# Self attention's projections as float16 pairs, with a reordered start and end, in a three-layer transformer block

## The reference, cut to what matters

```python
x = x + _L0_xattn_ref(_layernorm(x), ctx_1024, mask, rms_scale, q_w, kv_w, out_w)  # 32 x 64 rows, 512 wide
x = x + _L0_attn_ref(_layernorm(x), WQ, WK, WV, WO)
x = x + _L0_ffn_ref(_layernorm(x), W_fc, ln_w, ln_b, W_proj)
...
def _L0_attn_ref(x, WQ, WK, WV, WO):
    def heads(W): return (x @ W).reshape(B, S, 16, 32).transpose(0, 2, 1, 3)
    Q, K, V = (heads(WQ), heads(WK), heads(WV))
    score = causal softmax of einsum('bhqd,bhkd->bhqk', Q, K) / sqrt(32)
    out = einsum('bhqk,bhkd->bhqd', score, V)
    return out.transpose(0, 2, 1, 3).reshape(B, S, E) @ WO
```

## Time and profile before

| | us |
|---|---|
| median of 3 runs | 1067.03 (1064.93 to 1068.35) |
| profiled execution | 1066.37 |
| its span, first to last instruction | 1064.4 |
| TensorE busy, weight loads busy | 930.7, 700.7 |
| VectorE, ScalarE, GpSimd busy | 668.4, 505.0, 375.6 |

### The profile page before, as it was taken

How to read it: one execution, slowest core, us unless ns; L and a number is a source line. 1 busy time by engine, 2 the same in 40 slices (tenths; PEclk the granted TensorE clock), 3 DMA queues, 4 the chain that set the end, 5 groups by cost and what they waited for, 6 DMA issues and landing times. The chain is left out here.

```text
span 1064.4 us, 22549 instructions
## 1 busy us (share of the span) xinstructions
PE 930.7 (87%) x7307; PEld 700.7 (66%) x7307; DVE 668.4 (63%) x1334; ACT 505.0 (47%) x1059; POOL 375.6 (35%) x506
## 2 busy tenths in 40 slices
PE   3798879898888888878979999999889999999996
PEld 2787667686676776657968887888765444444443
DVE  5577756766766777676366566766656538475543
ACT  4565445654455554544333333433446455555542
POOL 3354444444444444440022111211103325444434
PEclk9899989999999999988989999999989999999998
DMA  6621223211222322331355543444422102012011
...
DMA packets 100318, 93.02 MB, mean 87 GB/s; under 512 B 45424, under 2 KB 61904, under 8 KB 100176
## 3 DMA queue, kind: packets, MB, share of 16 engines
...
q0 software_dynamic: 128, 0.03, 0.0%
...
## 5 line engine op out<-in xcount | busy, mean ns | idle before, releaser
L255 PE MATMUL bank<-f,f 128*128 128x256 f32 (+4 forms) x5032 | 637.8, 300 | 68.8 <-issue 26.0
L255 PEld LDWEIGHTS bank<-f,f 128*128 128x128 f32 (+3 forms) x5032 | 460.9, 160 | 196.5 <-issue 80.8
L244 DVE TENSOR_TENSOR f<-bank,f 128x512 fp32r<-128x512 f32 x211 | 140.5, 683 | 47.7 <-ACT f L241 45.8
L241 ACT ACTIVATE f<-bank 128x512 fp32r<-128x512 f32 x211 | 121.1, 591 | 88.8 <-PE bank L230 83.6
L230 PE MATMUL bank<-f,f 128*128 128x128 f32 x896 | 132.5, 279 | 33.7 <-DVE f L244 13.0
L230 PEld LDWEIGHTS bank<-f,f 128*128 128x128 f32 x896 | 102.9, 143 | 56.1 <-issue 31.3
L1248 PE MATMUL bank<-f,f 128*128 128x512 f16 x512 | 123.1, 384 | 0.0
L1221 POOL TENSOR_TENSOR f<-f,f 128x512 f32<-128x512 f32 x59 | 75.1, 1273 | 132.9 <-ACT f L1216 132.9
L1226 DVE SCALAR_TENSOR_TENSOR f<-bank,f,f 128x512 f16<-128x512 f32 x64 | 48.0, 750 | 92.0 <-ACT f L1208 75.8
L463 POOL TENSOR_TENSOR f<-f,f 128x512 f32<-128x512 f32 x32 | 42.0, 1311 | 160.9 <-ACTq L75 138.9
L954 POOL TENSOR_TENSOR f<-f,f 128x512 f32<-128x512 f32 x32 | 33.4, 1043 | 177.4 <-DVE f L951 177.4
...
## 6 DMA issues: line engine op xcount, KB each, us to landing
...
```

Source lines behind the costliest of these rows:

```text
L241: return maybe("act", lambda e: e.activation(hi, src, ACT.Copy), sem(name + "_hi"), waits, when)
L244: return maybe("dve", lambda e: e.tensor_tensor(lo, src, hi.bitcast(F32), ALU.subtract), sem(name + "_lo"), waits, when)
L255: f = lambda e, i=i, a=a, b=b: e.matmul(dst, a, b, start=(first and i == 0), stop=(last and i == n - 1), skip_group_check=check)
```

## The change

*Projections.* The pairs of WK, WQ, WV, WO, of the transposed x and of the attention result are float16 in place of float32r. Each weight is divided by its largest magnitude before it is split: `s2_wmax` reduces it on VectorE, `s2_wout` writes the 128 maxima to memory and `s2_wback` reads them back into every partition, `s2_wscale` takes the maximum and its reciprocal. Q and K are scaled back in ScalarE's copy out of PSUM (`s2_qk`), V times WO in `store`. `halves` is `split` without the bit cast; `s2_ET` uses it too. The split of WK moves from slots T0-6..T0-3 to T0-4..T0-1, the load of WO from B2+3 to T0+14.

*Start.* The squares of batches 0 to 2 move from three slots ahead of their tile's transpose to just behind it; the low part of the cross attention's Q weight moves from ahead of the slots into slots -1 and 0; Q2 and Q3 of pair 0 move from slots -3 and -1 to 1 and 3; the load of x for pair 1 moves from slot -4 to behind the first batch's loads; the first two masks are loaded behind the second batch's.

*End.* The last statistics stand ahead of all of the last two blocks' products, the sums of squares first; those products then run tile by tile.

The diff, without the passing of `wmaxd` (a 4x128 array in memory) from `program`, the `chunks` argument of `scaled_lo`, the type of `ET2` and its `halves`, and the removed line that emitted two of the last products ahead of the statistics:

```diff
             done["ssq", b] = done["sq"]
+            if b <= 2:
+                cx_free[b].append(done["sq"])
             tp = inv_sqrt("s_r", rr[:, b % 4, :], sst[:, b % 4, :], ss[:, b % 4, :],
...
         if j == FT - 1:
-            cx_free[b] = [tt, done["ssq", b]]
+            cx_free[b] = [tt, *([done["ssq", b]] if b > 2 else [])]
...
+    def first_masks():
+        for b in range(2):
+            done["msk", b] = load_mask(b)
     def stage_mask(b):
         u = b % 2
-        t = load_mask(b)
+        t = done["msk", b] if b < 2 else load_mask(b)
         done["bias", b] = [op("pool", lambda e: e.tensor_scalar(
...
     stage_Q1b(0)
-    tw1["q"] = scaled_lo(wq_t, WQh, WQl, [t_wq, t_r1], t_qh)
     side[0] = Q
     ahead = [(s, s.n) for s in sems.values()]
+    def stage_WQ(c):
+        tw1["q"] = scaled_lo(wq_t, WQh, WQl, [t_wq, t_r1], t_qh, [c])
     begun = [*begun, *(None if k.startswith("s_e_") else s.n for k, s in sems.items())]
     for c in range(4):
+        at(-1 + c // 2, 4, lambda c=c: stage_WQ(c))
         at(5 + c, 9, lambda c=c: stage_Wo(c))
     at(3, 9, load_wo)
+    at(-11, 2.65, first_masks)
     for b in range(nb):
...
         at(s0 - 6 if b > 2 else -11, 1.6 + b, lambda b=b: load_tab(b))
-        at(s0 + 4 if b > 0 else -1, 1.7, lambda b=b: stage_mask(b))
+        at(s0 + 4, 1.7, lambda b=b: stage_mask(b))
         for j in range(FT):
-            at(s0 - 5 + j, 0.3, lambda b=b, j=j: stage_square(b, j))
+            at(s0 - (5 if b > 2 else 2) + j, 0.3 if b > 2 else 1.5, lambda b=b, j=j: stage_square(b, j))
             at(s0 + j - 2, 1, lambda b=b, j=j: stage_T(b, j))
...
             if i:
-                at(s0 - 12, 1.4, lambda i=i: load_xq(i))
+                at(s0 - 12 if i > 1 else -11, 1.4 if i > 1 else 1.65, lambda i=i: load_xq(i))
                 at(s0 - 7, 1.4, lambda i=i: stage_Q0(i))
             if i:
                 at(s0 - 6, 8.1, lambda i=i: stage_Q1(i))
                 at(s0 - 5, 8, lambda i=i: stage_Q1b(i))
-            at(s0 - 3, 8, lambda i=i: stage_Q2(i))
-            at(s0 - 1, 8, lambda i=i: stage_Q3(i))
+            at(s0 - 3 if i else 1, 8, lambda i=i: stage_Q2(i))
+            at(s0 - 1 if i else 3, 8, lambda i=i: stage_Q3(i))
...
     for i in range(3):
-        Wh[i], Wl[i] = early(4, D, dt=F32R), early(4, D, dt=F32R)
-    XT = [early(2, 4, 256, dt=F32R), early(2, 4, 256, dt=F32R)]
+        early.at = CONST + (24576, 32768, 57344)[i]
+        Wh[i], Wl[i] = early(4, D, dt=F16), early(4, D, dt=F16)
+    early.at = CONST + 73728
+    XT = [early(2, 4, 256, dt=F16), early(2, 4, 256, dt=F16)]
+    early.at = CONST + 90112
     xa, xn = early(2, D), early(2, D)
-    Wh[3], Wl[3] = outs(4, D, dt=F32R), outs(4, D, dt=F32R)
+    Wh[3], Wl[3] = outs(4, D, dt=F16), outs(4, D, dt=F16)
     WO_raw = outs(4, D)
...
     mrow, mdiag, isc, sc, lsc = const(2), const(2), const(2), const(2), const(2, 16)
+    wmx, wis, wsc = const(4), const(4), const(5)
+    back = Region(CONST + EARLY + 72704, CONST + EARLY + 74752)(4, 128)
     tok, tW = {}, {}
...
+    def s2_wmax(i):
+        tok["wm", i] = op("dve", lambda e: e.tensor_reduce(
+            wmx[:, i:i + 1], raw_w(i).rearrange("p c n -> p (c n)"), AX.X, ALU.max, apply_absolute_value=True),
+            sem("s_wm"), [tok["w", i]])
+    def s2_wout(i):
+        tok["wo", i] = dma(wmaxd[i:i + 1, :].rearrange("a (p n) -> (a p) n", n=1), wmx[:, i:i + 1], f"s_wo{i}", [tok["wm", i]])
+    def s2_wback(i):
+        tok["wb2", i] = dma(back[:, i, :], wmaxd[i:i + 1, :].to_broadcast([128, 128]), f"s_wo{i}", [tok["wo", i]])
+    def s2_wscale(i):
+        D_ = lambda f, w: op("dve", f, sem("s_wm"), w)
+        t = D_(lambda e: e.tensor_reduce(wis[:, i:i + 1], back[:, i, :], AX.X, ALU.max), [tok["wb2", i]])
+        t = D_(lambda e: e.tensor_scalar(wis[:, i:i + 1], wis[:, i:i + 1], 1.0e-30, None, ALU.max), [t])
+        t = D_(lambda e: e.reciprocal(wsc[:, i:i + 1], wis[:, i:i + 1]), [t])
+        if i == 3:
+            t = D_(lambda e: e.tensor_tensor(wsc[:, 4:5], wis[:, 2:3], wis[:, 3:4], ALU.mult), [t])
+        tok["wsc", i] = t
     def s2_wsplit(i, after, c):
-        tW[i] = split("s_W2", raw_w(i)[:, c, :], Wh[i][:, c, :], Wl[i][:, c, :],
-                      [tok["w", i], *after()], [tok["w", i]])
+        src, hi, lo = raw_w(i)[:, c, :], Wh[i][:, c, :], Wl[i][:, c, :]
+        th = op("act", lambda e: e.activation(hi, src, ACT.Copy, scale=wsc[:, i:i + 1]), sem("s_W2_hi"),
+                [tok["wsc", i], *after()])
+        tl = op("dve", lambda e: e.scalar_tensor_tensor(lo, src, wsc[:, i:i + 1], hi, ALU.mult, ALU.subtract),
+                sem("s_W2_lo"), [th, tok["wsc", i]])
+        tW[i] = [th, tl]
+    def halves(name, src, hi, lo, w_hi, w_lo=()):
+        th = op("act", lambda e: e.activation(hi, src, ACT.Copy), sem(name + "_hi"), w_hi)
+        return th, op("dve", lambda e: e.tensor_tensor(lo, src, hi, ALU.subtract), sem(name + "_lo"), [th, *w_lo])
...
         tok["xnT", i] = [tt]
-        tok["XT", i] = split("n_XT", dst, dsth, dstl, [tt, *free])
+        tok["XT", i] = halves("n_XT", dst, dsth, dstl, [tt, *free])
         give(k, tok["XT", i])
     def store(i, dst_d, k, tk):
         u, j = i % 2, i % ni
-        to = op("dve", lambda e: e.tensor_tensor(xo[:, u, :], bank[k][:, :], xr[:, u, :], ALU.add),
-                sem("n_xo"), [tk, tok["xr", i], *tok["late"], *d2("ost", i - 2)])
+        to = op("dve", lambda e: e.scalar_tensor_tensor(xo[:, u, :], bank[k][:, :], wsc[:, 4:5], xr[:, u, :],
+                                                        ALU.mult, ALU.add),
+                sem("n_xo"), [tk, tok["xr", i], tok["wsc", 3], *tok["late"], *d2("ost", i - 2)])
         tok["out", i] = [to]
...
         o = (QT, KT)[which][:, u % 2, c, :]
-        tok["qk", u] = [op("act", lambda e: e.activation(o, bank[k][:, 0:256], ACT.Copy), sem("a_QK"),
-                           [tk, *tW[w], *tok["early"], *d2("sc", 2 * u - 3)])]
+        tok["qk", u] = [op("act", lambda e: e.activation(o, bank[k][:, 0:256], ACT.Copy, scale=wis[:, w:w + 1]), sem("a_QK"),
+                           [tk, tok["wsc", w], *tW[w], *tok["early"], *d2("sc", 2 * u - 3)])]
         give(k, tok["qk", u])
...
     at(T0 - 9, 0, s2_x)
-    at(T0 - 10, 2, lambda: s2_wload(0))
-    at(T0 - 6, 2, lambda: s2_wload(1))
-    at(T0 - 5, 2, lambda: s2_wload(2))
+    for i, s in enumerate((T0 - 10, T0 - 6, T0 - 5, T0 + 14)):
+        at(s, 2 if i < 3 else 8.8, lambda i=i: s2_wload(i))
+        at(s + 2, 9, lambda i=i: s2_wmax(i))
+        at(s + 3, 3, lambda i=i: s2_wout(i))
+        at(s + 4, 3, lambda i=i: s2_wback(i))
+        at(s + 6, 8.9, lambda i=i: s2_wscale(i))
     for c in range(4):
-        at(T0 - 6 + c, 9, lambda c=c: s2_wsplit(0, lambda: d("Q", ni - 1), c))
+        at(T0 - 4 + c, 9, lambda c=c: s2_wsplit(0, lambda: d("Q", ni - 1), c))
         at(T0 + 1 + c, 9, lambda c=c: s2_wsplit(1, lambda: done["kv", FT * nb - 1], c))
...
     at(T0 + 13, 8.9, s2_late)
-    at(B2 + 3, 8.7, s2_outs)
-    at(B2 + 3, 8.8, lambda: s2_wload(3))
+    at(T0 + 14, 8.7, s2_outs)
     for n in range(64):
...
     def s3_plast():
-        for t in (2, 3):
-            s3_p(last - 1, [t])
         for t in range(4):
-            s3_p(last, [t])
+            for q in (last - 1, last):
+                s3_p(q, [t])
     def s3_stat(g):
         v, k = g % 2, take()
-        w = [*tok["acc", g], *tok["acc2", g], *gfree[k], t_on]
-        for t in range(4):
-            for z in range(2):
+        w = {1: [*tok["acc2", g], *gfree[k], t_on], 0: tok["acc", g]}
+        for z in (1, 0):
+            for t in range(4):
                 rows = slice(t * 128, (t + 1) * 128)
                 parts = [acc[:, v, z, rows]] + ([sq3[:, last % 2, rows]] if z and g == ng - 1 else [])
                 for n, a in enumerate(parts):
                     tk = op("pe", lambda e, t=t, z=z, a=a, n=n, m=len(parts) - 1: e.matmul(
                         bank[k][:, z * 4 + t:z * 4 + t + 1], a, ones[:, 0:1], start=n == 0, stop=n == m,
-                        skip_group_check=True), sem("f_p") if t == 3 and z and n == len(parts) - 1 else None,
-                        w if t + z == 0 else ())
+                        skip_group_check=True), sem("f_p") if t == 3 and not z else None,
+                        w[z] if t + n == 0 else ())
         tok["stat", g] = [tk]
```

15 lines of the change are left out of this document (8 added, 7 removed).

## The result

The changed kernel takes 1078.31 us (median of 4 runs, 1075.47 to 1080.85) where the kernel before took 1066.64 beside it (4 runs). The recorded ratio is 1.0117, 95% interval 1.0098 to 1.0136; the two medians alone give 1.0109. It is slower by 1.1 to 1.2%. I had forecast 1050.0, with 1060 as the upper bound. The profiled execution took 1075.47 us, its span is 1073.5 us and its mean granted clock 0.965; before, 1066.37, 1064.4 and 0.970.

A forecast was written before the change was run, and what follows sets the result against it. It took TensorE to bound self attention and feed-forward. Projections -14, maxima +3.5 and +0.5, start -6, end -0.5 sum to -16.5 us from 1066.37: 1049.9, predicted as 1050.0 us, with 1038 to 1060 for 8 in 10.

The forecast's parts named there:

- Projections: Self attention: float16 groups save 21 us of TensorE time, of which 14 us are kept (7 to 21).
- Reductions: Passage to self attention: 2.3 us each on VectorE; +3.5 us on the path, plus 0.5 for the output weight.
- The small DMAs: SyncE's queue: the maxima's write makes Q and V weights some 3 us later; at nothing, up to 2 us.
- The start: First 45 us: early x for pair 1 removes 7 us of TensorE loss, 6 kept (2 to 8).
- the output weight's landing: Start: ScalarE would stall 4 to 5 us for the cross attention's output weight, about 4 us covered.
- WO's earlier load: Self attention's output weight loaded four slots earlier, its reduction hidden in VectorE's idle time; 0.5 us booked.
- The end: Last 20 us: statistics 0.7 us earlier, ahead of the last products; gain 0.5 us (0 to 0.8).
- (c): Passage: VectorE becomes the bound, reductions and landings waited for cost 18 us; 1073 us in all, chance 0.05.

The follow-up runs named there:

- run 4: The kernel before with only the edits to the first slots (squares, masks, x for pair 1, Q of pair 0); 1069.6 us, ratio 1.0034.
- run 7: The constant-scale kernel of run 3 with the load of WO back from slot T0+14 to B2+3; 1056.1 us, ratio 0.9907.
- run 3: The changed kernel with a constant scale of 16 for every weight, so no maxima, write or read back; 1061.7 us, ratio 0.9969.
- run 1: The changed kernel without the write of the maxima to memory and their read back, the four large reductions kept; 1065.9 us, ratio 0.9999.
- eleventh kernel: The constant-scale kernel of run 7 with the squares of batch 2 back at their old, early place; 1052.2 us, ratio 0.9879.
- run 5: The start-only kernel of run 4 with the squares of batch 2 back at their old place; 1063.2 us, ratio 0.9976.
- run 9: The start-only kernel of run 4 with pair 2's statistics of x queued on GpSimd behind r of batch 2; 1064.45 us, ratio 0.9988.
- eighth kernel: The changed kernel with each partition writing its maximum as 512 bytes instead of 4, one row read back; 1066.05 us, ratio 0.9994.

## Why the prediction was wrong

By the medians, a chain of single edits leads from before to after: 1065.7, + 3.9 (start, run 4), - 13.5 (projections and end, run 7 against run 4), + 5.6 (WO's place, run 3 against 7), + 4.2 (maxima, run 1 against 3), + 12.4 (round trip, after against run 1) = 1078.3 us. Each term carries 1 to 3 us of uncertainty, and they are not independent (taking the reductions out with the writes in place gives 6.6 in place of 4.2). Against it, point by point:

- **Projections, right.** I took 14 us kept, plus 0.5 for the end; the runs give 13.5 for both. The groups last 1.47 us (256 columns) and 2.75 us (512), where I expected 1.51 and 2.75. By the same reading as in the prediction a float16 matmul of 256 columns takes (1.47 - 0.277)/11 = 0.108 us (0.277 is the mean duration in after), not 0.111. TensorE's busy time fell by 16.5 us. Its idle time in 560 to 780 us rose from 15 us to 23.6 in the seventh and the eleventh kernel: the chains took their share, as the step said. The 64 scaled copies of Q and K on ScalarE, which I had at nothing, last 469 ns, 380 before; no wait for them is among the listed ones from 560 to 790 us of after.
- **Reductions, right in size.** 2276 ns each (2.3 predicted), 4.2 us on the path (4.0 predicted), at the places where I had it (3.9 and 0.8 for 3.5 and 0.5).
- **The small DMAs, the first step that failed.** "So at nothing, and up to 2 us" for SyncE's queue; measured 12.4 us. The number of steps and the queue behind them were in my sum, the transfer's own duration was not: I had no row of a 4-byte piece, and took a small transfer for a short one. The nearest row that I had, a megabyte's landing of 6.1 us, taken for each of the waits that SyncE makes in turn, would have given a far higher upper end; even that is short of the 8.3 us measured.
- **The start, the second step that failed.** -6 predicted, +3.9 measured. Two faults. The 5.87 us had more than one cause: with x early, 3.05 are left in run 4 and 5.87 in run 5; by the traces what is late there is r of batch 1 and the key rotation behind it. And I followed the moved squares only on ScalarE, never to their reader: r on GpSimd, then the keys' copy. Run 9 shows that this alone is 5 us. The 4 to 5 us that I feared from the output weight's landing do stand in after (ScalarE idle for 5.38 us until 45.72), but by run 9 and the first table little or nothing of the loss is theirs.
- **WO's earlier load, the third.** I booked 0.5 us, hidden under VectorE's idle time. Measured 5.6 by the medians, 3.9 in the two waits of run 7's traces, by its load ahead of the x tile's on one queue. I looked at the engine that the new work uses and not at the queue that its load shares.
- **The end, right.** From the last GELU to the end of the span before takes 19.0 us, after 18.5.
- **The rivals.** (c) gave 1073 us and was the nearest in time, which is luck for the most part. One piece of its mechanism stands in after, the 3.36 us in which WO's maximum holds VectorE until WO has landed. But all of VectorE's added work, with such a wait in it, costs 4.2 us (run 1 against 3) and not the 18 that (c) had, and the 12.4 us go with the narrow write. The range ended at 1060 because each failed step had its upper end too near: 2 us where 12 came, -2 where +3.9 came.

What stays open: the 5.6 us of WO's place and the 3.9 us of the start rest on medians; the profiled executions show 3.9 and 2.5. The 12.4 us of the round trip were not split into what the slow landings of the transfers beside the write cost and what SyncE's standing queue costs; the wide write shortens both. By the first table's events they fall in both parts of the passage: from the 13th sum to the 16th after takes 81.8 us and the eighth kernel 74.1, from there to the first store 41.4 and 38.9. Why 4-byte pieces to one stretch are slow, no run shows.
